# One VectorE product for two neighbouring units in a Mamba scan with a mixture of experts

## The reference

```python
def step(s, inp):
    d_t, u_t, B_t, C_t = inp
    dA = jnp.exp(d_t[..., None] * A)
    s = s * dA + (d_t * u_t)[..., None] * B_t[:, :, None, :]
    y_t = jnp.einsum('bhdn,bhn->bhd', s, C_t)
    return (s, y_t)
```

## Time and profile before

| | us |
|---|---|
| median of 3 runs | 1237.58 |
| lowest and highest of them | 1233.49, 1238.75 |
| the profiled execution, its time | 1234.84 |
| the profiled execution, its span | 1232.9 |

### The profile page before, as it was taken

One profiled execution on the slowest core, in us unless ns is written; L12 is line 12 of the kernel. 1 busy time (PEld: TensorE's weight loads), 2 busy tenths in 40 slices (PEclk: granted clock), 3 DMA queues, 4 the chain that ended last, 5 costly groups with the idle time before them and its releaser, 6 DMA issues.

```text
span 1232.9 us, 15308 instructions
## 1 busy us (share of the span) xinstructions
PE 1022.4 (83%) x3821; PEld 476.4 (39%) x3821; DVE 1070.5 (87%) x1331; ACT 734.7 (60%) x1117; POOL 858.9 (70%) x708
## 2 busy tenths in 40 slices
PE   0755858999999899999999997888888888888785
PEld 0522324444545454444445453333333333243322
DVE  7647968889898979899898989999898989999996
ACT  2564535767586776767685766556564756555421
POOL 2335788767676867677676769687777868686755
PEclk9988868999999999999999999788887979797765
DMA  6542325243432424342534423442434333343311
GB/s 160 157 94 68 91 79 130 57 99 69 107 80 64 103 62 111 77 94 51 119 68 98 89 57 80 86 86 48 87 71 90 81 73 68 82 85 80 72 36 34
DMA packets 81065, 103.01 MB, mean 84 GB/s; under 512 B 13280, under 2 KB 51072, under 8 KB 81024
## 3 DMA queue, kind: packets, MB, share of 16 engines
q1 hardware_dynamic: 76928, 94.18, 35.3%
q0 software_dynamic: 4096, 8.40, 2.3%
HBM read 18.66 MB, written 16.78 MB: 29 GB/s over the span
## 4 chain that ended last, share of the span: by engine, by line
PE 40%; DVE 24%; issue 22%; POOL 7%; ACT 3%; DVEq 1%; DMA 1%; SPq 1%; POOLq 0%; ACTq 0%
DVE u_sb L902 10%; DVE s_sb L972 8%; PE bank L1204 6%; PE bank L1171 5%; PE bank L1189 5%; PE bank L1127 4%; PE bank L1182 4%; PE bank L1114 3%; POOL expert_in L585 3%; PE bank L1135 2%; PE bank L1136 2%; PE bank L1137 2%; POOL s_sb L578 2%; PE bank L1147 2%; DVE g_sb L860 2%
## 5 line engine op out<-in xcount | busy, mean ns | idle before, releaser
L578 POOL TENSOR_TENSOR s_sb<-s_sb,c_of 128x512 f32<-128x512 f32 x480 | 628.5, 1315 | 273.2 <-DVE s_sb L972 265.1
L972 DVE TENSOR_TENSOR_SCAN s_sb<-bank,u_sb 128x512 f32<-128x512 f32 x512 | 620.4, 1212 | 0.0
L762 ACT ACTIVATE bank<-bank,a_neg 128x510 f32<-128x510 f32 x512 | 334.0, 659 | 255.9 <-PE bank L1189 246.4
L902 DVE TENSOR_TENSOR u_sb<-bank,b_of 128x512 f32<-128x512 f32 x512 | 346.2, 676 | 98.7 <-PE bank L1182 94.9
L1182 PE MATMUL bank<-dsp,sel_d 128*128 128x512 f32 x512 | 316.1, 617 | 39.8 <-DVE u_sb L902 20.4
L1189 PE MATMUL bank<-dsp,sel_d 128*128 128x512 f32 x512 | 244.5, 478 | 79.0 <-DVE s_sb L972 71.5
L1182 PEld LDWEIGHTS bank<-dsp,sel_d 128*128 128x128 f32 x512 | 104.6, 204 | 243.4 <-DVE u_sb L902 147.6
L1189 PEld LDWEIGHTS bank<-dsp,sel_d 128*128 128x128 f32 x512 | 106.5, 208 | 195.4 <-DVE s_sb L972 163.0
L1204 PE MATMUL bank<-s_sb,con 128*32 128x512 f32 x1024 | 161.2, 706 | 12.7 <-POOL s_sb L578 6.8
L1114 PE MATMUL bank<-xnT,wx 128*128 (+1 forms) x256 | 128.8, 597 | 0.0
L585 POOL DMA_INDIRECT expert_in<-xn,put_at x64 | 65.6, 1026 | 17.9 <-issue 17.8
(11 more groups left out here) (140 smaller groups left out, 1045.0 us busy)
## 6 DMA issues: line engine op xcount, KB each, us to landing
b_of<-bc SPq DMA_DIRECT2D x64, 256.0 KB
c_of<-bc SPq DMA_DIRECT2D x64, 256.0 KB
dsp<-hi SPq DMA_DIRECT2D x64, 256.0 KB
dsp<-dd SPq DMA_DIRECT2D x64, 256.0 KB
expert_in<-dd SPq DMA_DIRECT2D x8, 512.0 KB, 6.4
xn<-expert_in SPq DMA_DIRECT2D x8, 512.0 KB, 5.4
xn<-L_ffn_W SPq DMA_DIRECT2D x16, 256.0 KB, 4.6
expert_out<-xn SPq DMA_DIRECT2D x16, 256.0 KB, 2.4
```

What stands on the lines that cost most here:

```text
L578: pool.tensor_tensor(s_now, s_now, c_of[:, hf, hh, :], ALU.mult).then_inc(S["p_ready"], 1)
L762: act.activation(d, d, ACT.Exp, scale=a_neg[:, k:k + 1]).then_inc(S["decay_ready"], 1)
L902: dve.tensor_tensor(u_sb[:, w % U_RING, :], du_ps[w % 2][:, :], b_of[:, hf, head_of(w), :], ALU.mult).then_inc(S["u_ready"], 1)
L972: dve.tensor_tensor_scan(s_sb[:, w % S_RING, :], decay_of(w)[:, :], u_sb[:, w % U_RING, :], 0.0, ALU.mult, ALU.add).then_inc(S["scan_done" ...
```

## The change

du of two neighbouring units goes to one PSUM tile `du_pair` of two banks. In every even pass TensorE writes both halves, with the two matmuls one behind the other, and then delta of one unit; in odd passes it spreads delta alone. VectorE makes u of both units in one operation of 1024 elements, whose B operand is the same 512 elements twice. The pair is made after the scan of the even unit w, for the units w + 2 and w + 3, instead of one unit ahead of each scan. The du matmuls of a pair wait until the pair before has been multiplied. A wait for scan w - 1 stands ahead of the product, since the pair overwrites the place of units w - 2 and w - 1 in `u_sb`. All other work is where it was.

```diff
-        bank = [ctx.enter_context(nc.psum_tensor(f"bank{i}", [P, CH], F32)) for i in range(8)]
+        bank = [ctx.enter_context(nc.psum_tensor(f"bank{i}", [P, CH], F32)) for i in range(3)]
+        du_pair = ctx.enter_context(nc.psum_tensor("du_pair", [P, 2, CH], F32))
+        bank += [ctx.enter_context(nc.psum_tensor(f"bank{i}", [P, CH], F32)) for i in range(5, 8)]
         decay = bank[0:3]
-        du_ps = bank[3:5]
-        y_ps = bank[5]
-        misc = bank[6:8]
+        du_ps = [du_pair[:, k, :] for k in range(2)]
+        y_ps = bank[3]
+        misc = bank[4:6]
...
-                dve.wait_ge(S["du_spread"], per_chunk(ch, SLOTS, w + 1))
-                dve.tensor_tensor(u_sb[:, w % U_RING, :], du_ps[w % 2][:, :], b_of[:, hf, head_of(w), :], ALU.mult
-                                  ).then_inc(S["u_ready"], 1)
+                dve.wait_ge(S["du_spread"], per_chunk(ch, SLOTS, w + 2))
+                b_now = b_of[:, hf, head_of(w), :].unsqueeze(1).broadcast_to([P, 2, CH])
+                dve.tensor_tensor(u_sb[:, w % U_RING:w % U_RING + 2, :], du_pair[:, :, :], b_now, ALU.mult
+                                  ).then_inc(S["u_ready"], 2)
...
                 for w in range(SLOTS):
-                    if w + 1 < SLOTS:
-                        spread_u(ch, w + 1)
-                    elif ch[0] + 1 < CHUNKS:
-                        spread_u(after(ch), 0)
...
-                    dve.wait_ge(S["u_ready"], per_chunk(ch, SLOTS, w + 1))
+                    dve.wait_ge(S["u_ready"], per_chunk(ch, SLOTS, w // 2 * 2 + 2))
                     dve.tensor_tensor_scan(s_sb[:, w % S_RING, :], decay_of(w)[:, :], u_sb[:, w % U_RING, :], 0.0,
                                            ALU.mult, ALU.add).then_inc(S["scan_done"], 1)
+                    if w % 2 == 0:
+                        wait(dve, "scan_done", per_chunk(ch, SLOTS, w))
+                    if w % 2 == 0 and w + 2 < SLOTS:
+                        spread_u(ch, w + 2)
+                    elif w % 2 == 0 and ch[0] + 1 < CHUNKS:
+                        spread_u(after(ch), 0)
...
-                wait(pe, "u_ready", per_chunk(ch, SLOTS, w - 1))
-                pe.matmul(du_ps[w % 2][:, :], sel_d[:, group_of(w), :, :].rearrange("k n d -> k (n d)"),
-                          dsp[:, hf, head_of(w), 1, :], start=True, stop=True).then_inc(S["du_spread"], 1)
+                wait(pe, "u_ready", per_chunk(ch, SLOTS, w))
+                for k in range(2):
+                    pe.matmul(du_pair[:, k, :], sel_d[:, group_of(w + k), :, :].rearrange("k n d -> k (n d)"),
+                              dsp[:, hf, head_of(w), 1, :], start=True, stop=True).then_inc(S["du_spread"], 1)
...
             def spread(ch, w):
-                spread_du(ch, w)
+                if w % 2 == 0:
+                    spread_du(ch, w)
                 spread_delta(ch, w)
```

## The result

The changed kernel takes 1247.62 us in the median (1246.6 to 1247.77), against 1233.81 for the kernel before in the same comparison: a ratio of 1.0102, 95% interval 1.0084 to 1.0119. It is 1% slower, 13.8 us; the forecast was 1205, 33 us or 2.6% under the 1237.58 of the kernel before, with a range that ends at 1238. The profiled execution took 1247.77 us, of which 1245.8 are the span.

A forecast was written before the change was run, and what follows sets the result against it. No single engine was taken as the bound (TensorE 40% of the chain, VectorE 24%). Expert chunks 9.6 us, combining chunks 21.6 and chunk 15 1.5 to 2 made 33 us, giving 1205 us, range 1190 to 1238.

The forecast's parts named there:

- The fixed cost: On VectorE, one wide product instead of two u saves 0.04 to 0.05 us per pair, 12 us if VectorE bound throughout.
- The drain rule: Rival: VectorE's pipeline empties between operations, so a pair saves 0.15 us and the kernel takes 1187 us; chance 0.04.
- scan behind scan dearer: Rival, with a dearer wide product: 0.08 us per VectorE pair or more is lost, 1215 to 1235 us; chance 0.08.
- Behind it only VectorE's own pair is queued: On VectorE, the wait for scan w - 1 behind scan w costs nothing, since only the pair stands behind it.
- For even n this is the same place: VectorE asks for an even unit's du at the same point as before; odd units' u and du come one scan earlier.
- The order's gain: Asking for odd units' du earlier, with the pairs' saving, gains 1.2 us per expert chunk and 3.6 per combining chunk.
- step by step path of chunk 5: An expert chunk followed through its passes: gains of 0.9, then 1.7 us, part given back, 1.2 us in the end.
- a gate (0.6, as a u): In chunk 5's count of VectorE work up to scan 6, a gate was priced at 0.6 us, like a u.
- The waits for odd units: VectorE's waits for odd units' du go; before, du waits were 6.4 us per expert and 4.9 per combining chunk.
- du 16, a margin of 1.0 us: In chunk 5, the DMA for du 16 lands 0.4 us earlier and its pair is ready 1.0 us before VectorE asks.
- both banks held at once: Rival: refills can't overlap reads and odd scans release work 0.54 us later; 24 us lost, 1255 us; chance 0.14.
- What I said would prove me wrong: Signs: du waits staying 5 us per combining chunk, sums waiting for GpSimd in passes 10 and 14, TensorE clock below 0.85.

The follow-up runs named there:

- two_products: The changed kernel with two products of 512 elements, one per bank, at the pair's place, both du still waited for together; 1251.5 us.
- half_gate_out: gate_out_first with GpSimd's product with C over 256 of the 512 columns only; 1192.8 us.
- gate_out_first: The changed kernel with only the gates and the expert outputs moved ahead of the pair; 1232.0 us.
- half_before: The kernel before the change with GpSimd's product with C over 256 of the 512 columns only; 1217.4 us.
- pair_last: The changed kernel with the pair as the last VectorE operation of its even pass, all other work ahead of it; 1238.4 us.
- odd_late: pair_last with the gathered rows' adds in odd passes 17 to 31, ahead of the gate in pass 21, chunk 15 as it was; 1219.1 us.
- apart_gate_out: gate_out_first with two products of 512 elements, each with its own du wait and its bank refilled separately; 1231.1 us.
- before_late: The kernel before the change with the other VectorE work of every even pass put behind the u of the next pass; 1296.2 us.

## Why the prediction was wrong

- **The fixed cost: right, over-sized in its worth.** Pairs start 1.12 us before the scan behind them, scans 1.13 before the next. Two products in the pair's place start 0.59 and 0.60 us before what follows (two_products), so a pair saves 0.065 us, a little more than the 0.04 to 0.05 of the sum: 16.6 us of VectorE in 256 pairs, of which 3.8 show in the time. The drain rule, 0.15 us per pair, and "scan behind scan dearer" are out by the same distances.
- **"Behind it only VectorE's own pair is queued": the step that failed.** Gate 2, the expert output of pass 26, the split of pass 24 and the adds of even passes are queued behind it too. "For even n this is the same place" counted scans only: before, the other work of pass n - 2 ran ahead of u n; now it runs behind the pair and the pair's wait. I listed what waits *inside* the pair and not what stands behind it, and who waits for that. Its price: 13.6 us with half products (half_gate_out), 15.7 with whole ones (gate_out_first, where 7.5 us of stretch go as well).
- **The order's gain: about right, where it can be seen.** With the queue gone and GpSimd's products halved, the terms come out near the sum: 1.1 to 1.33 us per expert chunk (forecast 1.2) and 3.3 per combining chunk (3.6), 24.6 in all where the sum had 33. Whether the step by step path of chunk 5 is right in each of its steps wasn't followed. What lacks lies in chunks 1 and 2: together 136.2 us in half_before and 139.5 in half_gate_out, longer where I had them shorter. I didn't follow that.
- **"a gate (0.6, as a u)": mis-sized, and with it all small work.** I priced gates, splits and adds by their durations before, 666, 1218 and 329 ns, and moved them to a place where they take 1323, 1850 and 495. This term was absent from the sum and from the rivals; it is worth 20 to 25 us by the half products, the largest of the losses. The trace before shows the condition, had I looked at two engines together. In pass 14 of chunk 11 (VectorE, then GpSimd) the add starts at the scan's end, and GpSimd's product, which waits for the same scan, comes 0.16 us later; a pair between them turns the two round, as the add of pass 14 in the changed kernel shows with 0.6 to 0.9 us:

```profile
905.71 0.33 DVE L893 SCALAR_TENSOR_TENSOR acc<-xn,gate,acc 128x128 f32 x1
...
905.87 1.30 POOL L578 TENSOR_TENSOR s_sb<-s_sb,c_of 128x512 f32<-128x512 f32 x1 [0.19 <-DVE s_sb L972]
```

- **The waits for odd units: right in the combining chunks** (9.1 us in 8 waits, the longest 2.2, where I had at most 2). In the expert chunks they rose from 38.2 us in 36 waits to 50.3 in 32. TensorE is 91% busy there; that the waits only moved to the pairs is the likely reading, and no run isolates it.
- **"du 16, a margin of 1.0 us": wrong.** TensorE still waits for that DMA, 1.0 us in four of the chunks 3 to 8 (before, 0.8 in all six), and 1.2 us in each combining chunk, where it waited for none before. In the combining chunks of pair_last and odd_late, with the split at 1292 and 1196 ns instead of 1850, that wait is gone.
- **The rival "both banks held at once": real, mis-sized and mis-placed.** I gave it 24 us at 0.14. It costs 9.8 us in this order. With the gates and outputs ahead it costs less, some 4.7 by the estimate at apart_gate_out, which isn't nothing.
- **The ledger.** -24.6 (order and pair, alone, with half products) + 13.6 (queued work) + 24.8 (collision) = +13.8, the measured difference. The three are differences of medians in one sequence of edits, so that they add up to the measured difference by construction; in another sequence they share out a little differently (15.7 for the queue with whole products), and the last one holds whatever else the half product does.
- **What I said would prove me wrong didn't.** Waits for du stayed under 5 us per combining chunk, TensorE's sums waited for GpSimd in none of the chunks 10 to 14, and the granted clock rose from 0.85 to 0.87. None of the signs looked at the duration of work the change only moved. What did show it were the lengths: 69.2 us per chunk in chunks 3 to 8 (forecast 66.8), 68.6 in 10 to 14 (64.7), and 3.4 us more in chunk 0, which I had at nothing.

Open: why GpSimd's backlog still meets gate 2 in odd_late (851 ns instead of 666), and why the wide product with its held banks is 5 us behind two products there, while the two are level in gate_out_first's order.

## What to carry over

When an operation with a wait is moved or widened, write down the whole queue behind it on its engine, and for each entry who waits for it; put what others wait for ahead. An operation is priced for a place, not by its name: if all its operands are in SBUF, look up what GpSimd does at the new start time, and do so for the work behind it as well. Put such operations right behind one that GpSimd's work depends on, or beside an idle GpSimd. And measure the order apart from the instruction: here the best kernel has the new order and not the wide instruction.

## What the hardware showed that I had not expected

- A VectorE operation with all operands in SBUF doesn't end before a GpSimd product that was running at its start: an add of 0.33 us took 0.89 to 1.0 in one product and 3.07 across three, ending 0.15 us behind the last (906.46 against 906.30); a copy of 8 elements took 0.87 instead of 0.14 (before_late). The product keeps 1.27 to 1.30 us.
- The reverse, too: GpSimd's product that started 0.16 us after such an operation took 1.30 us instead of 1.27 behind an add, and one that started 0.27 us after a low split took 2.25 (pass 24 of chunk 11 in pair_last; the split itself, which met the product ahead, 1.39). Before the change it was more often GpSimd that paid: 35 of its 480 products took over 1.4 us, against 7 of 480 after.
- VectorE operations with one operand in PSUM show nothing of this in any of the runs.
- GpSimd shows as 68% busy and as a minor share of the chain, and yet it cost VectorE 20 us in five chunks. The loss stands in VectorE's busy time, in no row of waits.
